# The last attention of a fused four-layer kernel: exp's bias from one fused subtract-and-minimum over the scores

## The reference

```python
q = (x @ Wq + bq).reshape(1, B * N, H, hd)
kv = (cond @ Wkv + bkv).reshape(1, -1, 2, H, hd)
...
q = _fq_sym(q, axis=-1)          # step = max|q| / 127 of each token and head, rounded to whole steps
k = _fq_sym(k, axis=-1)
v = _fq_sym(v, axis=2)
attn = jnp.einsum('bhqd,bhkd->bhqk', q, k)
attn = jax.nn.softmax(attn.astype(jnp.float32), axis=-1)
attn = _fq_unsigned(attn, axis=-1)   # step = row maximum / 255
out = jnp.einsum('bhqk,bhkd->bhqd', attn, v)
```

## Time and profile before

| | us |
|---|---|
| median of 3 runs | 2987.26 (2987.25 to 2993.5) |
| the profiled execution | 2982.61 |
| its span | 2980.8 |
| DVE busy in the span | 2100.4 (70%) |
| PE busy | 2496.5 (84%) |
| ACT busy | 1644.0 (55%) |
| POOL busy | 531.2 (18%) |

### The profile page before, as it was taken

One profiled execution on the slowest core, in us unless ns is written; L12 is line 12 of the kernel. 1 busy time (PEld: TensorE's weight loads), 2 busy tenths in 40 slices (PEclk: granted clock), 3 DMA queues, 4 the chain that ended last, 5 costly groups with the idle time before them and its releaser, 6 DMA issues. The chain is left out here.

```text
span 2980.8 us, 51198 instructions
## 1 busy us (share of the span) xinstructions
PE 2496.5 (84%) x19929; PEld 1674.4 (56%) x19929; DVE 2100.4 (70%) x4548; ACT 1644.0 (55%) x2847; POOL 531.2 (18%) x401
## 2 busy tenths in 40 slices
PE   6969999988999786897887677777777777789999
PEld 5746676765666454674665444444444444456666
DVE  6857878774343586675758799999999999943231
ACT  4534545442333364443434688888888888822232
POOL 2224333321221233221311300000000000011121
PEclk9989999998999777999999899999999999989999
DMA  3120000002000212101013300000000000000000
GB/s 138 41 77 6 11 8 18 6 4 78 22 22 11 92 36 70 31 26 43 29 43 108 116 9 14 10 9 8 15 16 9 14 10 9 3 27 22 11 11 11
DMA packets 58943, 92.85 MB, mean 31 GB/s; under 512 B 5440, under 2 KB 54608, under 8 KB 57680
## 3 DMA queue, kind: packets, MB, share of 16 engines
q1 hardware_dynamic: 58704, 89.57, 9.0%
HBM read 66.48 MB, written 23.07 MB: 30 GB/s over the span
## 5 line engine op out<-in xcount | busy, mean ns | idle before, releaser
L2653 ACT ACTIVATE attend_ex<-psum,attend_mx,queries_step 128x1024 uint16<-128x1024 f32 x512 | 618.4, 1208 | 123.0 <-DVE attend_mx L2684 123.0
L2755 PEld LDWEIGHTS psum<-ident_b,attend_ex 128*128 128x128 bf16 x4096 | 253.7, 101 | 399.5 <-issue 398.3
L2755 PE MATMUL psum<-ident_b,attend_ex 128*128 128x128 bf16 x4096 | 330.3, 226 | 149.6 <-DVE attend_pw L2688 119.5
L2743 PE MATMUL psum<-keys_turned,queries_ahead 96*128 96x512 bf16 x1024 | 330.1, 407 | 75.3 <-ACT attend_ex L2653 71.8
L1502 PE MATMUL psum<-arena,moe_tokT 128*128 128x512 f32 (+2 forms) x896 | 361.6, 548 | 3.4 <-DVE moe_h L1389 3.4
L2677 DVE TENSOR_REDUCE attend_mx<-psum 128x1 f32<-128x512 f32 x512 | 329.4, 685 | 26.7 <-PE psum L2743 8.8
L2673 DVE TENSOR_REDUCE attend_mx<-psum 128x1 f32<-128x1024 f32 x256 | 310.9, 1215 | 6.3 <-PE psum L2743 5.9
L1389 DVE TENSOR_TENSOR moe_h<-moe_sg,psum 128x512 f32<-128x512 f32 (+1 forms) x112 | 69.9, 625 | 266.1 <-PE psum L1502 258.9
L1502 PEld LDWEIGHTS psum<-arena,moe_tokT 128*128 128x128 f32 x896 | 166.5, 192 | 139.9 <-issue 121.3
L1236 ACT ACTIVATE moe_sg<-psum 128x512 f32<-128x512 f32 (+1 forms) x112 | 61.4, 548 | 292.4 <-PE psum L1502 288.2
L2765 PE MATMUL psum<-values,attend_pw 128*128 128x16 f16 x4096 | 180.9, 171 | 1.4 <-DVE attend_pw L2688 0.6
(11 more groups left out here) (455 smaller groups left out, 4804.4 us busy)
## 6 DMA issues: line engine op xcount, KB each, us to landing
residual<-stored_rows SPq DMA_DIRECT2D x48, 128.0 KB, 1.7
queries_turned<-queries_rows SPq DMA_DIRECT2D x16, 384.0 KB, 3.1
queries_ahead<-queries_turned SPq DMA_DIRECT2D x16, 384.0 KB, 3.3
arena<-in_moe SPq DMA_DIRECT2D x1, 5704.0 KB, 18.2
arena<-in_gqa SPq DMA_DIRECT2D x1, 5440.0 KB, 18.0
arena<-in_moe SPq DMA_DIRECT2D x1, 4360.0 KB, 13.2
xatt_ct<-in_ctx_T SPq DMA_DIRECT2D x32, 128.0 KB, 2.1
residual<-stored_rows SPq DMA_DIRECT2D x16, 256.0 KB, 2.1
```

The costliest lines, as they stand in the source:

```text
L2653: nc.scalar.activation(ex[:, u % 4], S[:, u % 3], ACT.Exp, bias=mx[:, t % 2, h, 4:5], scale=steps[:, 0, t, h:h + 1], accum_out=sums[:, t % ...
L2743: last = nc.tensor.matmul(S[:, u % 3, b * 512:(b + 1) * 512], qt[:, t % 2, h * P:(h + 1) * P], KT[:, c:c + 4, h // 2], start=True, stop=True)
L2755: last = nc.tensor.transpose(TP[:, c], counts[u % 4][:, c * P:(c + 1) * P], k["ident_b"][:])
```

## The change

The bias is -step * max + ln 255, which is the minimum over the scores of (score + shift) * (-step) with shift = -ln 255 / step. The change computes it in that way.

- In `attend3`, `maximum(u)` now is `tensor_tensor_reduce`: (score + shift) * (-step), folded with minimum from a starting value. The even unit starts from 3.0e38, the first odd half from the even unit's result, the second from the first's. The last result is the bias itself, so `bias(u)` with its two instructions goes. Each of the three operations also writes its whole product to a new bfloat16 buffer `shifted`.
- Each odd half has a second wait, for the `unit_max` of the operation ahead of it; each even one from u = 2 has a second wait, for the `bias` of the row-head ahead.
- shift and -step are columns of `steps`, which gets a third plane; it is filled in `qkv3` by a new instruction on POOL, `shift(t)`, behind `rstd(t + 3)`. It waits for `recip`. DVE's reciprocal of tile t gets a wait for `shift(t - 2)`.

```diff
--- before.py
+++ after.py
@@ -29,6 +29,7 @@
 MAGIC = 12582912.0
 NEG = -1.0e30
 COUNT_UNIT = float(2 ** 24)
+LN255 = 5.541263545158426
 
 
 W_XATT0 = dict(wq=DC * D, wp=DC * D, wk=DC * D, wv=DC * D, bq=D, bk=D, bv=D, bp=D)
@@ -2272,7 +2273,7 @@
 
         s = semaphores(nc, k, "qkv3_", """
             padded weights_next x_loaded0 x_loaded1 x_loaded2 x_loaded3 c_loaded0 c_loaded1 c_loaded2 c_loaded3
-            e_loaded0 e_loaded1 e_loaded2 e_loaded3 q_stored0 q_stored1 stats mean var rstd normed xT_psum xT qk_psum qk amax step_max recip
+            e_loaded0 e_loaded1 e_loaded2 e_loaded3 q_stored0 q_stored1 stats mean var rstd normed xT_psum xT qk_psum qk amax step_max recip shift
             divided rounded q_step n_step q_placed kq k_hi k_r1 k_mid k_r2 k_lo v_psum v v_part v_range v_all v_scale v_recip v_divided v_done
             qT_psum qT kT_psum kT""")
         QP = k["psum"][:, 0:4, :].rearrange("p (j b) c -> p j (b c)", j=2)
@@ -2363,6 +2364,10 @@
                 pool.wait_ge(s["var"], t + 1)
                 nc.gpsimd.tensor_tensor(sm[:, t % 2, 1:2], sm[:, t % 2, 0:1], k["neg_half"][:], ALU.pow).then_inc(s["rstd"], 1)
 
+            def shift(t):
+                pool.wait_ge(s["recip"], t + 1)
+                nc.gpsimd.tensor_scalar(steps[:, 2, t], stp[:, t % 2, 2, 0:NH], -LN255 * HD ** 0.5, None, ALU.mult).then_inc(s["shift"], 1)
+
             def over_all():
                 pool.wait_ge(s["v_range"], 4)
                 nc.gpsimd.partition_all_reduce(vx[:, 2], vx[:, 0], P, RMAX).then_inc(s["v_all"], 1)
@@ -2375,6 +2380,7 @@
 
             for i in range(-3, B):
                 at(rstd, i + 3)
+                at(shift, i)
                 if i == -2:
                     clear_spent(nc, k)
                 if i == 8:
@@ -2461,6 +2467,8 @@
                 nc.vector.tensor_scalar(step[:, 0:NH], amax[:, 0:NH], 1.0 / 127.0, 1e-8 * HD ** 0.5, ALU.mult, ALU.max)
                 nc.vector.tensor_scalar(step[:, NH:], amax[:, NH:], 1.0 / 127.0, 1e-8, ALU.mult, ALU.max).then_inc(s["step_max"], 1)
                 dve.wait_ge(s["step_max"], t + 1)
+                if t >= 2:
+                    dve.wait_ge(s["shift"], t - 1)
                 nc.vector.reciprocal(inv, step).then_inc(s["recip"], 1)
                 nc.vector.tensor_scalar(steps[:, 0, t], step[:, 0:NH], HD ** -0.5, None, ALU.mult).then_inc(s["q_step"], 1)
                 nc.vector.tensor_scalar(steps[:, 1, t], step[:, 0:NH], HD ** -0.5, -1.0, ALU.mult, ALU.mult).then_inc(s["n_step"], 1)
@@ -2589,20 +2597,20 @@
     UN = 2 * NH
     NU = B * UN
     LAG = 4
-    LN255 = 5.541263545158426
     with ExitStack() as ctx:
         def sb(name, shape, dt=F32):
             return ctx.enter_context(nc.sbuf_tensor("attend3_" + name, shape, dt))
 
         s = semaphores(nc, k, "attend3_", """
             weights_next q_loaded0 q_loaded1 o_stored0 o_stored1
-            even_scores odd_scores unit_max row_max bias exped turned evacuated
+            even_scores odd_scores unit_max bias exped turned evacuated
             attended both row_recip probs_step scaled o_done""")
         S = k["psum"][:, 0:6, :].rearrange("p (u b) c -> p u (b c)", b=2)
         TPW = k["psum"][:, 6, :]
         TP = TPW.bitcast(BF16).rearrange("p (c m) -> p c m", m=P)
         O = k["psum"][:, 7, 0:D]
-        mx = sb("mx", [P, 2, NH, 6])
+        mx = sb("mx", [P, 2, NH, 3])
+        shifted = sb("shifted", [P, UK], BF16)
         sums = sb("sums", [P, 2, 2, NH])
         tot = sb("tot", [P, 2, 3, NH])
         ex = sb("ex", [P, 4, UK], U16)
@@ -2650,7 +2658,7 @@
                     act.wait_ge(s["bias"], u // 2 + 1)
                 if u >= 4:
                     act.wait_ge(s["turned"], u - 3)
-                nc.scalar.activation(ex[:, u % 4], S[:, u % 3], ACT.Exp, bias=mx[:, t % 2, h, 4:5], scale=steps[:, 0, t, h:h + 1],
+                nc.scalar.activation(ex[:, u % 4], S[:, u % 3], ACT.Exp, bias=mx[:, t % 2, h, 2:3], scale=steps[:, 0, t, h:h + 1],
                                      accum_out=sums[:, t % 2, u % 2, h:h + 1]).then_inc(s["exped"], 1)
 
             def evacuate(u):
@@ -2667,21 +2675,21 @@
         @block.vector
         def _(dve):
             def maximum(u):
+
                 t, h = u // UN, u % UN // 2
+                best, n_step, n_shift = mx[:, t % 2, h], steps[:, 1, t, h:h + 1], steps[:, 2, t, h:h + 1]
                 if u % 2 == 0:
                     dve.wait_ge(s["even_scores"], u // 2 + 1)
-                    nc.vector.tensor_reduce(mx[:, t % 2, h, 0:1], S[:, u % 3], X, ALU.max).then_inc(s["unit_max"], 1)
+                    if u >= 2:
+                        dve.wait_ge(s["bias"], u // 2)
+                    nc.vector.tensor_tensor_reduce(shifted[:], S[:, u % 3], n_shift.to_broadcast([P, UK]), n_step, 3.0e38,
+                                                   ALU.add, ALU.min, best[:, 0:1]).then_inc(s["unit_max"], 1)
                 else:
                     for b in range(2):
                         dve.wait_ge(s["odd_scores"], u - u % 2 + b + 1)
-                        nc.vector.tensor_reduce(mx[:, t % 2, h, 1 + b:2 + b], S[:, u % 3, b * 512:(b + 1) * 512], X, ALU.max).then_inc(s["unit_max"], 1)
-
-            def bias(u):
-                t, h = u // UN, u % UN // 2
-                dve.wait_ge(s["unit_max"], u // 2 * 3 + 3)
-                nc.vector.tensor_reduce(mx[:, t % 2, h, 3:4], mx[:, t % 2, h, 0:3], X, ALU.max).then_inc(s["row_max"], 1)
-                dve.wait_ge(s["row_max"], u // 2 + 1)
-                nc.vector.tensor_scalar(mx[:, t % 2, h, 4:5], mx[:, t % 2, h, 3:4], steps[:, 1, t, h:h + 1], LN255, ALU.mult, ALU.add).then_inc(s["bias"], 1)
+                        dve.wait_ge(s["unit_max"], u - u % 2 + b + 1)
+                        nc.vector.tensor_tensor_reduce(shifted[:, 0:512], S[:, u % 3, b * 512:(b + 1) * 512], n_shift.to_broadcast([P, 512]), n_step, best[:, b:b + 1],
+                                                       ALU.add, ALU.min, best[:, b + 1:b + 2]).then_inc(s["bias" if b else "unit_max"], 1)
 
             def evacuate(u):
                 dve.wait_ge(s["turned"], u + 1)
@@ -2715,7 +2723,6 @@
                 if t and at == LAG:
                     scale_rows(t - 1)
                 maximum(u + 1)
-                bias(u + 1)
                 if u >= 4:
                     evacuate(u - 3)
                 if t and at == 2:
@@ -3304,7 +3311,7 @@
             KT = kept.enter_context(nc.sbuf_tensor("keys_turned", [96, B, NH // 2, P], BF16))
             V = kept.enter_context(nc.sbuf_tensor("values", [P, B, D], F16))
             v_step = kept.enter_context(nc.sbuf_tensor("values_step", [P, D], F32))
-            steps = kept.enter_context(nc.sbuf_tensor("queries_step", [P, 2, B, NH], F32))
+            steps = kept.enter_context(nc.sbuf_tensor("queries_step", [P, 3, B, NH], F32))
             q_rows = kept.enter_context(nc.sbuf_tensor("queries_rows", [96, 2, NH * P // 2], F32))
             q_ahead = kept.enter_context(nc.sbuf_tensor("queries_ahead", [96, 2, NH * P], BF16))
             qkv3(nc, k, res[0], ctx_T, qT, steps, KT, V, v_step, arena[0], nothing, hand(6, 8, 10), q_rows, q_ahead)
```

## The result

The changed kernel takes 3044.96 us (median of 4, 3038.07 to 3049.97) against 2987.26. The ratio is 1.0185, 95% interval 1.0169 to 1.0201. It is slower by 58 us, where 22 were forecast, and it lies above the stated range.

A forecast was written before the change was run, and what follows sets the result against it. DVE was taken to bound the last attention but for 0.16 us a row-head. Steady row-heads +16.6, tile ends +4.5, half clock -0.2 and projections +1.2 gave +22.1 us: 2982.6 to 3004.7 profiled, median 3009, range 2976 to 3034.

The forecast's parts named there:

- What bounds the kernel: Last attention: DVE bounds the 3.54 us row-head but for 0.16, ACT follows it, PE has slack.
- PE's 0.16: Ahead of the odd unit's first half: 0.16 of the 1.30 us is DVE waiting for PE's scores; the change swallows it.
- The fused operation: Attention maxima on DVE: 1.28 us for the even unit, 0.80 for each half, including 55 and 52 ns for scalars.
- the first rival: Attention's fused operations: scalars from memory cost less; no charge gives 2939 us (11%), one charge an instruction 2981 (11%).
- The read of the accumulator: Behind each fused operation in the attention: the read overlaps and costs 0.01 us.
- The wait of its own: Ahead of each odd half: the second wait, on `unit_max`, becomes an instruction of its own and costs 0.10 us.
- The sum of a row-head: Steady attention row-head: 0.48 + 1.39 + 1.75 = 3.62 us, 0.08 more; +16.6 us over 208 of them.
- Tile ends: 15 tile ends of the last attention, two row-heads each: +0.30 us each, +4.5 us together.
- Half clock: 18 attention row-heads with PE at half clock: only the 1.76 from first half to exp changes, -0.2 us.
- The projections: `shift` on POOL delays `over_all` and the norm DVE awaits: +1.2 us, 2 at most.
- the second rival: Ahead of the odd halves: waits cost nothing since an operation flushes anyway; row-head 3.34 us, time 2939; 3%.
- the element at two cycles: Attention's fused operations: two cycles an element, 2.1 us more in a row-head, time near 3550; 4%.

The follow-up runs named there:

- experiment 3: Changed kernel with immediates for both scalars from memory in all three fused operations, and a small immediate scale for exp; 2960.62 us, ratio 0.9901.
- experiment 4: Kernel before with a second, long satisfied wait put first ahead of L2682 and L2684, no work changed; 3030.87 us, ratio 1.0135.
- experiment 5: Kernel with three stock maxima and a fused operation over 3 elements, plus a satisfied wait ahead of that operation's one wait; 2977.08 us, single execution.
- experiment 6: Odd halves merged into one operation over 1,024 scores: in the changed kernel 2945.63 us, ratio 0.985; in the kernel before, stock form, 3026.15 us, ratio 1.0113.

## Why the prediction was wrong

- **What bounds the kernel** was right: the loop from exp over the scores and DVE's chain back to exp. DVE swallowed PE's 0.16 as forecast; PE isn't the releaser of the first half in a steady row-head any more. One reading was off: the earlier trace rows counts the exps of both units, and its last start, 2612.8, is an odd unit's. The even ones span 925.2 us and not 927.0, so 22.5 and not 24.3 us stood above the steady time, 14.6 of them at the tile ends (whose second row-head takes 3.76 and not 3.70) and 8.0 elsewhere. That moves the forecast by less than 1 us.
- **The fused operation** was right: 1.28 and 0.80 forecast, 1.274 and 0.809 measured. The charge for scalars from memory, the first rival, was settled by experiment 3, at 59 ns each and not 55 and 52. The halves' 0.009 more is 0.02 us in a row-head, 5 us in all.
- **The read of the accumulator** was right at 0.01.
- **The wait of its own** is the step that failed. The prediction took 0.10 for each half from a stock operation. The two stock operations of experiment 4 do pay 0.10, the fused one pays 0.146 (experiments 3 and 5). Twice 0.045 in 255 row-heads are 23 us of the 36 that were missed. The mechanism was right, its size was off, and the row was of another kind of operation. The kernel before has no fused operation behind such a wait that ends last; I should have put this price among the unknown ones with an upper bound, as I did for the operation itself.
- **The sum of a row-head**: 3.62 forecast, 3.73 measured. The 0.11 that is missing is 0.09 of gap and 0.02 of duration, 28 us over 255.
- **Tile ends**: +4.5 forecast for their 30 row-heads, +7.5 measured (0.18 for the first and 0.31 for the second of a tile end, where 0.06 and 0.24 were forecast).
- **Half clock**: -0.2 forecast. Such a row-head went from 4.16 to 4.22, the 0.06 by which the way from the first half to exp grew (1.76 to 1.82). There were more of them, too (23 for 13 outside the tile ends), and nothing in the prediction provides for that. Why is open. Over the whole stage, what stands above 255 steady row-heads grew by 6.0 us, where the forecast has 0.5 (its 20.9 for the stage less 255 x 0.08). The half clock's part of this swings from one execution to another.
- **The projections**: +1.2 forecast. The shift took 0.76 and not 0.55, its wait 0.70, and the place in the queue cost 1.6. Nothing shows the remainder of the 5.4 between the two profiled executions to be the change's: stages and runs without it swing as far.
- **The waits cost nothing** (the second rival) fell, and so did the element at two cycles: the slope is 1.04 ns an element, from 809 for 512 to 1344 for 1,024 with two scalars (experiment 6).

## What to carry to other kernels

Where a chain of short dependent instructions is the bound, count what stands between them, not their number: a wait that goes along with an instruction cost 0.036 us here, a wait of its own that ends last 0.10 ahead of the stock operations of experiment 4 and 0.146 ahead of a fused one, and the order of two `wait_ge` lines decides which of them it is. Put first the wait that ends last. The fused form paid most here where it replaced two short dependent steps on three elements (3.37 us a row-head), about as well as a chain of two long operations (3.38), and lost as a chain of three: 3.73 with waits that stood alone, and 3.60 with both orders swapped, still more than the 3.54 of the kernel before.

## What was not expected of the hardware

- The fused VectorE operation starts 0.084 to 0.086 us behind the end of a wait instruction ahead of it that ended last, the two stock ones of experiment 4 0.044 and 0.048. Size, memory and scalars play no part (experiments 3 and 5). Behind a wait that it carries itself it starts as soon as a stock one, 0.037.
- The trace of the kernel before has more stock operations behind such a wait: 80 TENSOR_TENSOR of L1389 at 0.044 to 0.045, 15 TENSOR_REDUCE of L907 at 0.043 to 0.049, 8 SCALAR_TENSOR_TENSOR of L3018 at 0.044 to 0.045. But three BATCH_NORM_STATS2 (L1762, L2436, L2985), each the first of its stage on VectorE, have 0.084 to 0.086, and single ones that open a stage 0.086 and 0.092 (L870, L405). So the larger figure isn't the fused operation's alone, and what causes it is open.
- At 1,024 elements from PSUM, writing a bfloat16 copy of everything, it takes 1215 ns with immediates, no more than the maximum that writes one value (1214).
